# ScalarE's feed-forward work takes other places in the last two row pairs; three VectorE steps move one slot; a class token's energy is written per group

## The chip, the cores and the metric

The kernel runs on one core of one Trainium2 chip. The metric is the device time of one execution in microseconds (us), lower is better. Engines are named TensorE (PE, its weight loads PEld), VectorE (DVE), ScalarE (ACT), GpSimd (POOL) and SyncE (SP, which here only issues DMAs). Each runs its own instructions in order and meets the others at semaphores.

## What is computed

One block of a vision tower over 16 images of 3 x 256 x 256. Sobel magnitudes, summed over the three colours, make 256 tokens of 256 numbers per image; a class token is put in front (S = 257). Then come attention, in which only the 27 tokens of highest energy are queries, and a feed-forward with quantized weights and codes and a depthwise convolution along the tokens.

```python
Ix, Iy = dwconv(x, kx), dwconv(x, ky)             # 3x3 Sobel
h = sum over colours of hypot(Ix, Iy)             # (16, 256, 256)
h = concat([cls_tok, h], axis=1)                  # (16, 257, 256)

z = layernorm(h)                                  # attention
energy = norm(z, axis=-1); _, idx = top_k(energy, 27)
ctx = softmax(q[idx] @ k.T / 4) @ v
result = mean(z, axis=1) everywhere, ctx @ out_w.T + out_b at idx
h = h + result

z = layernorm(h)                                  # feed-forward
g = quantized(z) @ quantized(w1).T                # 257 x 1024 per image
y = silu(depthwise_conv1d(g, conv_w) + conv_b)    # 3 taps along the tokens
h = h + quantized(y) @ quantized(w2).T
```

## The kernel before

**Staging.** The images go in four groups of four (`GB`, `GROUPS`). A group's magnitudes are made in four pairs of rows, i = 0 to 3 (`magnitude_rows`, L797 on VectorE, L1269 on ScalarE). While the magnitudes of group g are made, group g-1 goes through attention (pairs 0 and 1), the residual and the token codes (pair 2) and the feed-forward (pairs 2 and 3). Then VectorE quantizes the hidden values (`ffn_quantize`, L957), normalizes group g (`norm_mean`, `norm_tokens`) and adds the feed-forward's result. There are three such rounds, g = 1, 2, 3; group 0 before them and the last group's attention and feed-forward behind them run without a partner. A round takes about 351 us.

**A pair.** VectorE's part is a long row of steps over 128 x 768 numbers, f = 0 and f = 1 in turn (`hypotenuse`, L678). ScalarE does the absolute values (L1283, L1291, semaphore `mags`), the squares (L1316), the reciprocal roots (L1322, `recips`), the square of the quotient (L1328, `hisq`), the second reciprocal root (L1334, `halfrecip`), and two more squares (L1339, L1344). VectorE waits for each: for `mags` at the pair's start, for `recips` in front of its slot 1 arithmetic, for `hisq` at L746, for `halfrecip` at L753, for L1339's at L759 and for L1344's at L776. In pairs 1 to 3 the gradients are summed by GpSimd's accumulating DMAs (`carried_sums`, L490, the last one L518), which are set off by VectorE's and ScalarE's steps in the pair before.

**Slots.** Between these steps both engines call `slot(k)`, k = -2 to 8 on VectorE and -2 to 9 on ScalarE; other work is put there by hand. On ScalarE slots -2 and -1 stand ahead of the absolute values in pairs 1 to 3, slot 0 ahead of L1316, 1 and 2 behind L1322, 3 and 4 behind L1328, 5 behind L1334, 6 behind L1339, and 7, 8, 9 behind L1344.

**Feed-forward.** An image has 8 tiles of hidden channels, a group 32, numbered i = 0 to 31. TensorE multiplies tile i into PSUM (L1729, here g_i), ScalarE copies it into one of four `gpad` buffers (L1388, the *scale* step, here s_i), TensorE convolves it (L1717, conv_i), ScalarE takes the sum into `ydw` with its bias (L1395, the *take* step, t_i), and after the 8 takes of an image b ScalarE applies silu over all of them (`silu`, L1373, here a_b), whose semaphore `f_ready` VectorE's `hidden_maxima` (L953) waits for. TensorE's order is g_0 to g_3, then conv_0, g_4, conv_1, g_5 and so on: g_i needs s_(i-4), conv_i needs s_i and t_(i-4); s_i needs g_i and conv_(i-4). `FFN_SLOTS` (L38) says in which slot of pair 2 (first table) and pair 3 (second) ScalarE does which of them; an entry is (scale steps, image for silu, take steps). The silu of image 3 stands behind the whole of pair 3 (L1612). Silu and the reciprocal root need different function tables; where they alternate, a table load stands in front of the instruction.

**Attention in pair 1.** VectorE's `own_heads` (L1061) of image 1 is in slot -1. TensorE then picks the image's queries (L1869), and `context` (L1066) copies them at L1069; with it stand `shares` of image 2 and `queries` of image 3. TensorE's last transposes of image 2 (L1850) wait for that copy, and image 3's scores (L1833) wait for them through ScalarE (L1491) and for `queries`.

**Energies.** `select` (L998) finds the 27 highest energies of each image from a row `topk[:, 0, :]`. SP fills it by way of DRAM (L444 to L455): columns 1 to 256 for each group, column 0, the class token's, only for group 0. The row lies in `nrows_mem`, which also holds negated image rows.

Of the kernel before, what the change touches and what calls it, by code (L numbers as in the profile page):

```python
# [22 lines left out]
ACT = mybir.ActivationFunctionType  # L23
# [10 lines left out]
S = H + 1  # L34
# [1 line left out]


FFN_SLOTS = (  # L38
# [6 lines left out]


TILE_SLOTS = tuple((2 * k, 2 * k + 1) for k in range(8)) + ((),)
# [1 line left out]
GB = 4  # L49
# [10 lines left out]
FT = FF // P  # L60
# [66 lines left out]
def tower_kernel(nc, x, cls_tok, w_in, b_qk, b_v, w_out, b_out, w1, conv_w, conv_b, w2, const, out):  # L127
# [11 lines left out]
    with ExitStack() as ctx:  # L139
# [33 lines left out]
        cb = sb("cb", [P, FT])  # L173
# [14 lines left out]
        topk = nrows_mem[0:GB, 0:5 * S].rearrange("p (k n) -> p k n", k=5)  # L188
# [20 lines left out]
        take, again = arena("arena1", 18 * CH * W)  # L209
# [15 lines left out]
        take, again = arena("arena2", FT * ROW9 * P)  # L225
# [37 lines left out]
        gpad = sb("gpad", [P, 4, S + 2])  # L263
# [144 lines left out]
        @block.sync  # L408
        def _(sp):
            def load_weights():  # L410
                sp.dma_start(win[:, :, :], w_in.rearrange("(t p) n -> p t n", p=P)).then_inc(weights_in, 16)
                sp.dma_start(wout[:, :, :], w_out.rearrange("(t p) n -> p t n", p=P)).then_inc(weights_in, 16)

            for b in range(0, GB, 2):
                load_rows(sp, 0, b, 0, 3, img_first)
            sp.dma_start(cst[:, :], const).then_inc(table_in, 16)
            for b in range(0, GB, 2):
                load_rows(sp, 0, b, 3, 4, img_second)
            for b in range(GB):
                load_rows(sp, 0, b, 4, ROWS, img_in)  # L420
                load_rows(sp, 0, b, ROWS, ROWS + 2, img_in)
            sp.dma_start(h9[:, ROWS, :], cls_tok[0:1, :].to_broadcast([P, D])).then_inc(const_in, 16)
            sp.dma_start(stage.rearrange("p (t n) -> p t n", t=DT),
                         w1.rearrange("(t p) n -> p t n", p=P)).then_inc(w1_in, 16)
            sp.dma_start(stage2.rearrange("p (t n) -> p t n", t=FT),
                         w2.rearrange("(t p) n -> p t n", p=P)).then_inc(w2_in, 16)
            load_weights()
            sp.dma_start(bin_col[:, :], b_qk).then_inc(const_in, 16)
            sp.dma_start(bv_col[:, :], b_v).then_inc(const_in, 16)
            sp.dma_start(bo_row[:, :], b_out[0:1, :].to_broadcast([P, D])).then_inc(const_in, 16)  # L430
            sp.dma_start(cw[:, :, :], conv_w).then_inc(const_in, 16)
            sp.dma_start(cb[:, :], conv_b).then_inc(const_in, 16)

            def group(g, first=False, last=False):
                if first:
                    sp.wait_ge(stencil_psum, 2 * ROWS - 3)
                elif not last:
                    sp.wait_ge(mags, g * (2 * PAIRS) + 2 * PAIRS)
                if not last:
                    load_images(sp, g + 1)  # L440
                if not first:

                    sp.wait_ge(f_ready, g * GB)
                    load_weights()  # L444
                if first:

                    sp.wait_ge(e_ready, 1)
                    sp.dma_start(ec_dram, e9[0:1, ROWS:ROW9]).then_inc(e_out, 16)
                    sp.wait_ge(e_out, 16)
                    sp.dma_start(topk[:, 0, 0:1], ec_dram.to_broadcast([GB, 1])).then_inc(erow_in, 16)  # L450

                sp.wait_ge(e_ready, g + 1)
                sp.dma_start(e_dram, e9[:, 0:ROWS]).then_inc(e_out, 16)
                sp.wait_ge(e_out, g * 16 + 32)
                sp.dma_start(topk[:, 0, 1:S], e_dram.rearrange("(b r) j -> b (r j)", b=GB)).then_inc(erow_in, 16)  # L455
                if not first:
                    store(g - 1)

                sp.wait_ge(slots_ready, g + 1)
                sp.dma_start(s_dram.rearrange("(b r) j -> b (r j)", b=GB), topk[:, 4, 1:S]).then_inc(slots_out, 16)  # L460
                if not first:

                    sp.wait_ge(out_done, g * OUT_DONE)
                sp.dma_start(c_dram.rearrange("(b r) o -> b (r o)", b=GB), clsslot[:, :]).then_inc(slots_out, 16)
                sp.wait_ge(slots_out, g * 32 + 32)
                sp.dma_start(slot9[:, 0:ROWS], s_dram).then_inc(slot9_in, 16)
                sp.dma_start(slot9[:, ROWS:ROW9], c_dram).then_inc(slot9_in, 16)

            def store(g):

                sp.wait_ge(out_ready, g + 1)
                for b in range(GB):
                    sp.dma_start(out[bass.ds(g * GB + b, 1), 1:S, :].rearrange("o (p r) d -> (o p) r d", r=ROWS),
                                 out9[b * BLK:(b + 1) * BLK, 0:ROWS, :]).then_inc(out_done, 16)
                sp.dma_start(out[bass.ds(g * GB, GB), 0, :], out9[0:P:BLK, ROWS, :]).then_inc(out_done, 16)

            group(0, first=True)
            for g in range(1, GROUPS - 1):
                group(g)
            group(GROUPS - 1, last=True)  # L480
            store(GROUPS - 1)
            sp.wait_ge(out_done, GROUPS * OUT_DONE)
# [63 lines left out]
        def _(dve):  # L546
# [451 lines left out]
            def select(step, g):  # L998

                er, ew, tk, eq, slot = (topk[:, k, :] for k in range(5))  # L1000
                gt, cum = tk, ew
                dve.wait_ge(erow_in, g * 16 + 32)
                src = er
                for k in range(4):
                    settle()
# [130 lines left out]
            def slots_1(step, g):  # L1136
                def slot(k):
                    if k == -2: score_maxima(step, g, 2)
                    if k == -1: own_heads(step, g, 1)
                    if k == 0:  # L1140
                        context(step, g, 1)
                        shares(step, g, 2)
                        queries(step, g, 3)
                    if k == 2: score_maxima(step, g, 3)
                    if k == 3: own_heads(step, g, 2)
                    if k == 4:
                        context(step, g, 2)
                        shares(step, g, 3)
                    if k == 7: own_heads(step, g, 3)
                    if k == 8: context(step, g, 3)  # L1150
                return slot
# [89 lines left out]
        def _(act):  # L1241
# [136 lines left out]
                act.wait_ge(f_ready, gf * GB + b + 1)  # L1378
                s.activation(idle[:, half:half + 1], clsT[:, 0:1], ACT.Copy)

            def ffn_take(gf, scale, image, take):

                nt = gf * (GB * FT)
                for i in scale:
                    if i >= 4:
                        act.wait_ge(conv_psum, nt + i - 3)
                    act.wait_ge(g_psum, nt + i + 1)
                    s.activation(gpad[:, i % 4, 1:S + 1], (A0, A1, B0, B1)[i % 4][:, 0:S], ACT.Copy).then_inc(gd_ready, 1)  # L1388
                if image is not None:
                    act.wait_ge(conv_taken, nt + (image + 1) * FT)  # L1390
                    silu(gf, image, image % 2)
                for i in take:
                    t = i % FT
                    act.wait_ge(conv_psum, nt + i + 1)
                    s.activation(ydw[:, t, :], (C0, C1, T0, T1)[i % 4][:, 0:S], ACT.Identity,  # L1395
                                 bias=cb[:, t:t + 1]).then_inc(conv_taken, 1)

            def tap_diagonals(tiles):

# [168 lines left out]
            def slots_2(g):  # L1568
                def slot(k):
                    if k == 0: residual_sums(g)  # L1570
                    if k == 1:
                        tokens_scaled(g)
                        tap_diagonals(range(4, FT))
                    if k in FFN_SLOTS[0]:
                        ffn_take(g, *FFN_SLOTS[0][k])
                return slot

            def slots_3(g):
                def slot(k):
                    if k in FFN_SLOTS[1]:  # L1580
                        ffn_take(g, *FFN_SLOTS[1][k])
                return slot

            for lo, hi_, landed in ((0, 3, img_first), (3, 4, img_second)):
# [21 lines left out]
            for g in range(1, GROUPS):  # L1606
# [2 lines left out]
                magnitude_rows(g, 1, slots_1(gl))  # L1609
                magnitude_rows(g, 2, slots_2(gl), lambda: residual_squares(gl))  # L1610
                magnitude_rows(g, 3, slots_3(gl))
                ffn_take(gl, (), GB - 1, ())  # L1612
                norm_squares(lambda j: ln[0][:, j, :], d_ready, g, ROWS)
                ffn_scales(gl)
                first_root(g, ROWS)
# [352 lines left out]
```

## Time and profile before

| | |
|---|---|
| median of 3 runs | 1550.82 us (1550.23 to 1552.83) |
| profiled execution, device time | 1551.41 us |
| profiled execution, span | 1549.6 us |
| VectorE busy | 1319.3 us (85%) |
| TensorE matmul busy | 819.3 us (53%), weight loads 647.0 us |
| ScalarE busy | 718.5 us (46%) |
| GpSimd busy | 167.4 us (11%) |

The profile is one execution; the span runs from its first to its last instruction, 1.8 us less than the device time around it. Busy shares are means over stages with different limits, so they only say where to look. A line of the waits has the waiting engine and line, what released it, the us in total, how often, and the longest. A line of the timeline has the start, the us up to the last end of the run of like instructions, engine, line, operation, output and input, and in brackets how long the engine sat idle before it and what ended that. Neighbouring instructions overlap by some 0.1 us, so from start to start is a little less than a duration. On TensorE each fp32 multiplication of the program stands as two in the records, so "x6" at L1717 is one convolution (3 taps) and "x4" at L1729 one g_i. A line of the windows view has a stretch, its length, the busy us and instructions of PE, PEld, DVE, ACT and POOL, the granted TensorE clock as a share of 2.4 GHz, the share of the DMA engines and GB/s. Most times below are of the middle round, g = 2.

### The profile page before, as it was taken

To read this page: it belongs to the slowest core of one execution; us is meant where nothing else is said; L and a number is where in the kernel's file an instruction comes from. 1 tells how busy PE (TensorE), PEld (TensorE's weight loads), DVE (VectorE), ACT (ScalarE), POOL (GpSimd) and SP (SyncE) were. 2 spreads that over 40 slices of the span, in tenths; PEclk is the share of its full clock that TensorE was granted. 3 is DMA by queue.
4 is the path that set the end of the run, shared out by engine and by line. 5 is a ranking of instruction groups with operands and counts; after the bars stand their busy time and mean duration, and the time that the engine had idled before them with its cause. 6 is when DMAs were issued, how large, how long until landed. Compare 5 with 4: busy or idle time off the path is not lost.

```text
span 1549.6 us, 11187 instructions
## 1 busy us (share of the span) xinstructions
PE 819.3 (53%) x3334; PEld 647.0 (42%) x3334; DVE 1319.3 (85%) x2024; ACT 718.5 (46%) x1294; POOL 167.4 (11%) x208
## 2 busy tenths in 40 slices
PE   3465100467647733556648643456648633586534
PEld 1233000345546522445537533345537532475423
DVE  7999998898996999998997899998998799522576
ACT  2212242255486534255475644156476544243662
POOL 0000000022313000012303000012303000000000
PEclk8787555757679876667679876567579876688876
DMA  8000600034717510125618510116527010100001
GB/s 201 3 11 14 116 0 0 1 60 76 120 25 127 103 41 0 28 48 89 103 33 133 106 41 1 28 31 105 92 44 130 7 41 1 28 1 1 0 0 27
DMA packets 46356, 78.13 MB, mean 50 GB/s; under 512 B 7466, under 2 KB 31706, under 8 KB 44634
## 3 DMA queue, kind: packets, MB, share of 16 engines
q0 software_dynamic: 33408, 50.34, 20.0%
q1 hardware_dynamic: 12314, 26.31, 7.4%
q10 hardware_dynamic: 576, 0.79, 0.2%
q8 instruction: 26, 0.43, 0.1%
q14 instruction: 32, 0.26, 0.1%
HBM read 22.84 MB, written 4.25 MB: 17 GB/s over the span
## 4 chain that ended last, share of the span: by engine, by line
DVE 45%; ACT 14%; PE 13%; issue 8%; DMA 5%; POOL 0%; SPq 0%; DVEq 0%; ACTq 0%
DVE arena L564 15%; DVE arena L567 13%; ACT arena L1376 3%; DVE arena L953 3%; PE psum L1717 2%; PE psum L1811 2%; DMA arena<-nrows_mem 2%; DMA arena<-zT 2%; ACT arena L1249 2%; PE psum L1833 1%; DMA arena<-img 1%; DVE red L580 1%; ACT arena L1513 1%; PE psum L1786 1%; PE psum L1729 1%
## 5 line engine op out<-in xcount | busy, mean ns | idle before, releaser
L564 DVE TENSOR_TENSOR arena<-arena 128x768 f32<-128x768 f32 (+2 forms) x519 | 475.9, 968 | 58.2 <-ACT arena L1291 50.8
L567 DVE SCALAR_TENSOR_TENSOR arena<-arena 128x768 f32<-128x768 f32 (+2 forms) x224 | 201.5, 949 | 0.1
L1729 PE MATMUL psum<-zT,w1q 128*128 128x257 f32 x512 | 138.8, 405 | 21.0 <-DVE gpad L948 16.0
L1729 PEld LDWEIGHTS psum<-zT,w1q 128*128 128x128 f32 x512 | 103.0, 204 | 43.4 <-DVE gpad L948 20.9
L1717 PE MATMUL psum<-gpad,win 128*128 128x257 f32 x288 | 78.3, 411 | 47.8 <-ACT gpad L1388 47.8
L1833 PE MATMUL psum<-arena 128*128 128x257 f32 x128 | 55.0, 604 | 90.5 <-ACT arena L1491 72.1
L540 POOL DMA_DIRECT2D h<-others x60 | 51.5, 859 | 436.6 <-DVE others L567 357.0
L1328 ACT ACTIVATE arena<-arena 128x768 f32<-128x768 int16 x32 | 27.0, 844 | 154.1 <-DVE arena L567 153.7
L1717 PEld LDWEIGHTS psum<-gpad,win 128*128 128x128 f32 x288 | 57.4, 205 | 63.7 <-ACT gpad L1388 53.8
L1249 ACT ACTIVATE arena<-arena 128x256 f32<-128x256 f32 x65 | 23.3, 409 | 127.2 <-DVE arena L567 68.2
L1833 PEld LDWEIGHTS psum<-arena 128*128 128x128 f32 x128 | 36.8, 301 | 102.5 <-ACT arena L1491 75.8
L567 DVE SCALAR_TENSOR_TENSOR arena<-img 128x768 f32<-128x768 f32 x74 | 67.4, 948 | 9.1 <-DMA img<-x 8.7
L501 POOL DMA_DIRECT2D arena<-nrows_mem x18 | 15.6, 865 | 505.3 <-ACT arena L1300 433.0
L953 DVE TENSOR_REDUCE arena<-arena 128x288 f32<-128x2304 f32 (+1 forms) x16 | 64.3, 4078 | 0.1
L1395 ACT ACTIVATE xT<-psum,cb 128x257 f32<-128x257 f32 x96 | 42.7, 477 | 38.0 <-PE psum L1717 38.0
L1481 ACT ACTIVATE arena<-psum,arena 128x257 f32<-128x257 f32 x64 | 29.5, 474 | 65.3 <-DVE arena L1052 65.3
L1717 PE MATMUL psum<-gpad,onehotT 128*128 128x257 f32 x216 | 55.7, 400 | 7.5 <-ACT gpad L1388 7.5
L567 DVE SCALAR_TENSOR_TENSOR arena<-arena,others 128x768 f32<-128x768 int16 x64 | 58.2, 950 | 0.0
L1861 PE MATMUL psum<-arena 128*128 128x64 f32 x256 | 56.6, 362 | 2.8 <-ACT arena L1491 2.8
L1664 PE MATMUL psum<-img,cst 128*128 128x512 f32 (+1 forms) x28 | 16.0, 713 | 74.1 <-DVE arena L567 63.4
L1376 ACT ACTIVATE arena<-xT 128x2048 f32<-128x2048 f32 (+1 forms) x14 | 55.0, 3932 | 0.3
L1777 PE MATMUL psum<-cst,arena 128*128 128x128 f32 x64 | 15.6, 408 | 73.3 <-DVE e L564 71.2
(235 smaller groups left out, 2109.6 us busy)
## 6 DMA issues: line engine op xcount, KB each, us to landing
arena<-nrows_mem POOLq DMA_DIRECT2D x36, 384.0 KB, 7.7
arena<-img POOLq DMA_DIRECT2D x36, 384.0 KB, 7.6
img<-x SPq DMA_DIRECT2D x36, 258.0 KB, 7.0
h<-others POOLq DMA_DIRECT2D x60, 128.0 KB, 2.7
arena<-arena POOLq DMA_DIRECT2D x18, 384.0 KB, 8.8
arena<-zT POOLq DMA_DIRECT2D x12, 384.0 KB, 8.4
out<-out SPq DMA_DIRECT2D x16, 256.0 KB
img<-x SPq DMA_DIRECT2D x48, 64.5 KB, 6.7
```

Source lines behind the costliest of these rows:

```text
L540: pool.dma_start(h9[:, row, :], others[:, row % 2, c, :], accum_op=ALU.add).then_inc(row_sums, 16)
L564: return v.tensor_tensor(o, a, b, op)
L567: return v.scalar_tensor_tensor(out=o, in0=a, scalar=s, in1=b, op0=op0, op1=op1)
L953: return v.tensor_reduce(fmax[:, :, bass.ds(b, 1), :].rearrange("p j o r -> p j (o r)"), f4[:, :, :, bass.ds(b, 1), :].rearrange("p t j o ...
L1249: ins = s.activation(ln[1][:, j, :], src(j), ACT.Square)
L1376: s.activation(fb[:, :, 0:ROWS, :], yd[:, :, 1:S].rearrange("p t (r j) -> p t j r", j=ROWS), ACT.Silu)
L1395: s.activation(ydw[:, t, :], (C0, C1, T0, T1)[i % 4][:, 0:S], ACT.Identity, bias=cb[:, t:t + 1]).then_inc(conv_taken, 1)
L1717: ins = mm((C0, C1, T0, T1)[i % 4][:, 0:S], diagonal(t, k), gpad[:, i % 4, k:k + S], start=(k == 0), stop=(k == 2))
L1729: ins = mm((A0, A1, B0, B1)[i % 4][:, 0:S], w1q[:, k, t * P:(t + 1) * P], zT[:, k, b, :], start=(k == 0), stop=(k == DT - 1))
L1811: ins = mm(C0[:, t * P:(t + 1) * P], y_row(j)[:, t * P:(t + 1) * P], rhs, start=(j == 0), stop=(j == ROWS))
L1833: mm((C0, C1, T0, T1)[hg][:, 0:S], qbd[:, hg // 2, 4 * (hg % 2):4 * (hg % 2) + 4, :].rearrange("p h q -> p (h q)"), kT[:, b % 2, hg // 2, ...
L1861: mm(B1[:, chans], attnT[:, f, m, cols], V[:, b % 2, m, chans], start=(m == 0), stop=False)
```

## The change

1. `FFN_SLOTS` becomes a written order of single steps ("s13 t10 s14 ..."), and `ffn_take` goes through it. Of pair 2, slot 5 is empty now and slot 9 too; by its end 13 scale and 10 take steps are done, where it was 16 and 14. Of pair 3, slots -2, -1 and 0 are empty; slot 1 has six tiles and the silu of image 1, slot 3 four tiles, slot 6 three tiles, slot 7 the rest with the silu of images 2 and 3. The call behind pair 3 is gone, since `a3` is in slot 7.
2. On VectorE in pair 1, `context` of image 1, `shares` of image 2 and `queries` of image 3 move from slot 0 to slot 1, behind eight steps of the pair.
3. SP writes the class token's energy into column 0 for every group, ahead of the DMA that sends the other energies; `select` waits for both.

```diff
--- before.py
+++ after.py
@@ -36,12 +36,10 @@
 
 
 FFN_SLOTS = (
-    {2: ((0, 1, 2, 3), None, ()), 3: ((4, 5), None, (0, 1)), 4: ((6,), None, (2, 3)), 5: ((7,), None, (4, 5)),
-     6: ((8, 9), None, (6, 7)), 7: ((10, 11), 0, (8, 9)), 8: ((12, 13), None, (10, 11)), 9: ((14, 15), None, (12, 13))},
-    {-2: ((), None, (14, 15)), -1: ((), 1, ()),
-     0: ((16, 17), None, ()), 1: ((18, 19), None, (16, 17)), 2: ((20, 21, 22), None, (18, 19)),
-     3: ((23,), None, (20, 21, 22)), 4: ((24,), None, (23,)), 6: ((25, 26), 2, (24,)),
-     7: ((27, 28, 29), None, (25, 26)), 8: ((30, 31), None, (27, 28, 29)), 9: ((), None, (30, 31))})
+    {2: "s0 s1 s2 s3", 3: "t0 s4 t1 s5 t2 s6", 4: "t3 s7", 6: "t4 s8 t5 s9 t6 s10", 7: "t7 s11 a0", 8: "t8 s12 t9"},
+    {1: "s13 t10 s14 t11 s15 t12 s16 t13 s17 t14 s18 t15 a1", 3: "t16 s19 t17 s20 t18 s21 t19 s22",
+     6: "t20 s23 t21 s24 t22 s25",
+     7: "t23 a2 s26 t24 s27 t25 s28 t26 s29 t27 s30 t28 s31 t29 t30 t31 a3"})
 
 
 TILE_SLOTS = tuple((2 * k, 2 * k + 1) for k in range(8)) + ((),)
@@ -447,9 +445,9 @@
                     sp.wait_ge(e_ready, 1)
                     sp.dma_start(ec_dram, e9[0:1, ROWS:ROW9]).then_inc(e_out, 16)
                     sp.wait_ge(e_out, 16)
-                    sp.dma_start(topk[:, 0, 0:1], ec_dram.to_broadcast([GB, 1])).then_inc(erow_in, 16)
 
                 sp.wait_ge(e_ready, g + 1)
+                sp.dma_start(topk[:, 0, 0:1], ec_dram.to_broadcast([GB, 1])).then_inc(erow_in, 16)
                 sp.dma_start(e_dram, e9[:, 0:ROWS]).then_inc(e_out, 16)
                 sp.wait_ge(e_out, g * 16 + 32)
                 sp.dma_start(topk[:, 0, 1:S], e_dram.rearrange("(b r) j -> b (r j)", b=GB)).then_inc(erow_in, 16)
@@ -999,7 +997,7 @@
 
                 er, ew, tk, eq, slot = (topk[:, k, :] for k in range(5))
                 gt, cum = tk, ew
-                dve.wait_ge(erow_in, g * 16 + 32)
+                dve.wait_ge(erow_in, g * 32 + 32)
                 src = er
                 for k in range(4):
                     settle()
@@ -1137,7 +1135,7 @@
                 def slot(k):
                     if k == -2: score_maxima(step, g, 2)
                     if k == -1: own_heads(step, g, 1)
-                    if k == 0:
+                    if k == 1:
                         context(step, g, 1)
                         shares(step, g, 2)
                         queries(step, g, 3)
@@ -1378,22 +1376,23 @@
                 act.wait_ge(f_ready, gf * GB + b + 1)
                 s.activation(idle[:, half:half + 1], clsT[:, 0:1], ACT.Copy)
 
-            def ffn_take(gf, scale, image, take):
+            def ffn_take(gf, work):
 
                 nt = gf * (GB * FT)
-                for i in scale:
-                    if i >= 4:
-                        act.wait_ge(conv_psum, nt + i - 3)
-                    act.wait_ge(g_psum, nt + i + 1)
-                    s.activation(gpad[:, i % 4, 1:S + 1], (A0, A1, B0, B1)[i % 4][:, 0:S], ACT.Copy).then_inc(gd_ready, 1)
-                if image is not None:
-                    act.wait_ge(conv_taken, nt + (image + 1) * FT)
-                    silu(gf, image, image % 2)
-                for i in take:
+                for what, i in [(w[0], int(w[1:])) for w in work.split()]:
                     t = i % FT
-                    act.wait_ge(conv_psum, nt + i + 1)
-                    s.activation(ydw[:, t, :], (C0, C1, T0, T1)[i % 4][:, 0:S], ACT.Identity,
-                                 bias=cb[:, t:t + 1]).then_inc(conv_taken, 1)
+                    if what == "s":
+                        if i >= 4:
+                            act.wait_ge(conv_psum, nt + i - 3)
+                        act.wait_ge(g_psum, nt + i + 1)
+                        s.activation(gpad[:, i % 4, 1:S + 1], (A0, A1, B0, B1)[i % 4][:, 0:S], ACT.Copy).then_inc(gd_ready, 1)
+                    elif what == "t":
+                        act.wait_ge(conv_psum, nt + i + 1)
+                        s.activation(ydw[:, t, :], (C0, C1, T0, T1)[i % 4][:, 0:S], ACT.Identity,
+                                     bias=cb[:, t:t + 1]).then_inc(conv_taken, 1)
+                    else:
+                        act.wait_ge(conv_taken, nt + (i + 1) * FT)
+                        silu(gf, i, i % 2)
 
             def tap_diagonals(tiles):
 
@@ -1572,13 +1571,13 @@
                         tokens_scaled(g)
                         tap_diagonals(range(4, FT))
                     if k in FFN_SLOTS[0]:
-                        ffn_take(g, *FFN_SLOTS[0][k])
+                        ffn_take(g, FFN_SLOTS[0][k])
                 return slot
 
             def slots_3(g):
                 def slot(k):
                     if k in FFN_SLOTS[1]:
-                        ffn_take(g, *FFN_SLOTS[1][k])
+                        ffn_take(g, FFN_SLOTS[1][k])
                 return slot
 
             for lo, hi_, landed in ((0, 3, img_first), (3, 4, img_second)):
@@ -1609,7 +1608,6 @@
                 magnitude_rows(g, 1, slots_1(gl))
                 magnitude_rows(g, 2, slots_2(gl), lambda: residual_squares(gl))
                 magnitude_rows(g, 3, slots_3(gl))
-                ffn_take(gl, (), GB - 1, ())
                 norm_squares(lambda j: ln[0][:, j, :], d_ready, g, ROWS)
                 ffn_scales(gl)
                 first_root(g, ROWS)
```

## Rows read from the trace of the kernel before

**Rows 1.** The page's first part: busy time, share of the span, instructions.
```profile
PE 819.3 (53%) x3334; PEld 647.0 (42%) x3334; DVE 1319.3 (85%) x2024; ACT 718.5 (46%) x1294; POOL 167.4 (11%) x208
```

**Rows 2.** VectorE's waits over the whole span: total, times, longest.
```profile
DVE arena L564 <- ACT arena L1291: 50.8, 7, 16.1
DVE arena L1069 <- PE psum L1869: 31.2, 7, 5.7
```

**Rows 3.** VectorE's timeline, pair 3 and what follows: start, length, line, idle before.
```profile
858.63 3.56 DVE L564 TENSOR_TENSOR arena<-arena 128x768 f32<-128x768 f32 x4 [16.10 <-ACT arena L1291]
...
885.64 1.82 DVE L567 SCALAR_TENSOR_TENSOR arena<-arena 128x768 f32<-128x768 f32 x2
...
897.69 1.82 DVE L564 TENSOR_TENSOR arena<-arena 128x768 f32<-128x768 f32 x2 [1.22 <-ACT arena L1344]
...
910.71 11.99 DVE L953 TENSOR_REDUCE arena<-arena 128x288 f32<-128x2304 f32 x3
```

**Rows 4.** ScalarE's timeline over the end of pair 2 and pair 3.
```profile
840.54 0.82 ACT L1395 ACTIVATE xT<-psum,cb 128x257 f32<-128x257 f32 x2
...
851.99 3.87 ACT L1376 ACTIVATE arena<-xT 128x2048 f32<-128x2048 f32 x1
...
879.67 1.71 ACT L1328 ACTIVATE arena<-arena 128x768 f32<-128x768 int16 x2 [8.44 <-DVE arena L567]
...
886.62 1.71 ACT L1334 ACTIVATE arena<-arena 128x768 f32<-128x768 f32 x2 [2.52 <-DVE arena L567]
...
890.77 1.28 ACT L1376 ACT_TABLE_LOAD   x1
892.07 3.96 ACT L1376 ACTIVATE arena<-xT 128x2048 f32<-128x2048 f32 x1
...
896.47 0.46 ACT L1395 ACTIVATE xT<-psum,cb 128x257 f32<-128x257 f32 x1
...
908.59 3.94 ACT L1376 ACTIVATE arena<-xT 128x2048 f32<-128x2048 f32 x1
```

**Rows 5.** TensorE's timeline in pair 3, and last one stretch of the windows view.
```profile
859.65 2.94 PE L1717 MATMUL psum<-gpad,win 128*128 128x257 f32 x6 [7.33 <-ACT gpad L1388]
862.38 1.92 PE L1729 MATMUL psum<-zT,w1q 128*128 128x257 f32 x4
864.10 2.29 PE L1717 MATMUL psum<-gpad,win 128*128 128x257 f32 x6
866.22 1.03 PE L1729 MATMUL psum<-zT,w1q 128*128 128x257 f32 x4
867.09 1.46 PE L1717 MATMUL psum<-gpad,win 128*128 128x257 f32 x6
...
859.00:865.00 6.00, 5.35 (x13) 4.24 (x14) 6.00 (x9) 5.97 (x11) 0.00 (x0) 0.50 0.84 180
```

**Rows 6.** Timeline: GpSimd's last accumulating DMA for pairs 2 and 3, its user in pair 2.
```profile
771.28 0.86 POOL L518 DMA_DIRECT2D arena<-nrows_mem  x1 [1.18 <-DMA arena<-zT]
...
836.75 0.86 POOL L518 DMA_DIRECT2D arena<-nrows_mem  x1 [1.34 <-DMA arena<-h]
...
779.70 0.84 ACT L1291 ACTIVATE arena<-arena 128x768 f32<-128x768 f32 x1 [1.05 <-DMA arena<-nrows_mem]
```

**Rows 7.** Timelines of VectorE, ScalarE and TensorE in pair 1.
```profile
721.40 0.23 DVE L1069 COPY arena<-psum 128x64 f32<-128x64 f32 x1 [4.72 <-PE psum L1869]
...
734.25 1.22 DVE L1051 TENSOR_REDUCE arena<-psum 128x4 f32<-128x1028 f32 x1
...
719.67 1.58 ACT L1291 ACTIVATE arena<-arena 128x768 f32<-128x768 f32 x2
...
730.14 3.79 PE L1833 MATMUL psum<-arena 128*128 128x257 f32 x8 [7.43 <-ACT arena L1491]
```

**Rows 8.** SP's column-0 DMA (one line's answer: ns min/median/max), and select in the tail.
```profile
L450 SPq DMA_DIRECT2D nrows_mem<-ec_dram x1: 243/243/243, 270.0 to 270.0; - x1
...
1328.85 0.41 DVE L1006 MAX8 best<-nrows_mem 4x8 f32<-4x257 f32 x1
```

## The prediction

> **What bounds the kernel now.** First the busy times [rows 1]: VectorE works 85% of the span and no other engine much over half, so an edit pays mainly where VectorE stands still. Then VectorE's waits, longest in total first [rows 2]. At the top stands its wait for L1291, the absolute values at the start of a pair: 50.8 us in seven waits, the longest 16.1. Then VectorE's timeline over pair 3 [rows 3]: it sits idle for 16.10 us before it starts at 858.63. The same wait of 16.10 us stands in front of pair 3 in each of the three rounds, 48.3 of the 50.8 us. What ScalarE does meanwhile is in its timeline [rows 4]: take steps from 840.54 that wait for TensorE, then the silu of image 1 from 851.99, and only then the absolute values that VectorE wants. Pair 3 itself has one more wait, 1.22 us at 897.69, behind the silu of image 2 (892.07) that stands ahead of L1344. So in each round some 17 us of VectorE's time hang on where ScalarE's feed-forward steps stand, and the reader should see that this work isn't too much for ScalarE, it stands in the wrong place for VectorE.
>
> **Pair 2 to pair 3.** In the new order ScalarE has, behind the silu of image 0 (unmoved, done where the takes at 840.54 start [rows 4]), only t8, s12 and t9, at some 0.36 us each: 896.47 to the next step is such a take. It is free at about 841.7. What comes last then is GpSimd's sum. In pair 2 its last DMA was issued at 771.28 and its user began at 779.70 with no other cause to wait, 8.42 us later [rows 6]. The one for pair 3 is issued at 836.75 [rows 6], and nothing of the edit reaches it, since its inputs come from slots 4 to 6 of pair 2 and six short steps in slot 6 (2.1 us) end before L1344 is due. So the second absolute value starts at 845.17 and VectorE has it at 846.05. Before, the second step of VectorE's run began one step of 0.87 behind 858.63, at 859.50 [rows 3]. VectorE is **13.45 us** earlier. All times below marked "new" carry this shift, in the middle round.
>
> **Slot 1 of pair 3.** It begins when L1316, a table load of 1.28 and L1322 are done: maximum ready at new 846.9, squares to 847.8, load to 849.1, roots to 850.8 (a pair of such steps takes 1.7, as at L1334 [rows 4]). TensorE has stood since about 845.7 for want of s13 (s12 gave it conv_12 and g_16, again at the lower clock, from 841.4). What it does after such idle time is in its timeline [rows 5]: conv 2.73 from start to start, g 1.72, conv 2.12, then 0.87 and 1.30 (a record of 1.46 overlaps the next by 0.16). The granted clock over those six us is 0.50, the lower level of 1.2 GHz, after an idle time of 7.33 us [rows 5]; the steps that follow at half the length are at 2.4. The long steps cost 3.1 us over the steady pace of 2.17 a tile. conv_13 starts 0.4 behind s13, at 851.2; conv_15 ends 8.74 later at 859.9; t15 and the silu of image 1 with its load follow (890.77 to 896.47, 5.7 us [rows 4]), to 866.1. VectorE's quotient, and with it L1328, was at 879.67, new 866.22 [rows 4]: just in time, and its answer is not due before VectorE's 885.64, new 872.2 [rows 3]. Four microseconds of cover; hidden.
>
> **Slots 3 and 6.** ScalarE leaves L1328 at 867.9. Six of the eight steps find TensorE's work done (conv_18 and g_22 end by 867.3); t19 waits for conv_19, started on s19, to 870.2, and s22 ends at 870.9. The table load that the silu of image 1 has made necessary ends at 872.2. L1334 is due at 886.62 - 13.45 = 873.17 [rows 4]. Cover 1.0 us, the thinnest place: every us that TensorE takes over my 3.1 falls on VectorE. In slot 6 the silu is gone, six steps are done at 878.8, and L1344 isn't due before VectorE's L772, which ended at 896.47 (897.69 less 1.22 [rows 3]), new 883.0 for the second half. The 1.22 us wait goes too. VectorE's first maximum, which ends at 910.71 [rows 3] and takes 4.03, begins at 906.68, so VectorE's pair 3 ends at new 906.68 - 13.45 - 1.2 = 892.0.
>
> **Slot 7 and the last silu.** This is where part of the gain is given back. L1344 leaves ScalarE at 883.8. t23 and the silu of image 2 take 6.1, so s26 starts at 889.9 and TensorE, idle again for 5 us, starts conv_26 at 890.3. Behind it stand g_30, conv_27, g_31 and conv_28 to 31: 2.73 + 1.72 + 2.12 + 0.87 + 4 x 1.30 = 12.64 us [rows 5], to 903.0. t31 ends at 903.5, and the silu of image 3 without a load takes 4.3 (3.94 [rows 4] and the class token's 0.4): 907.8. VectorE's first three maxima take 4.03 each [rows 3] and end at 904.1. It waits 3.8 us, and the fourth ends at 911.9. Before, it ended at 910.71 + 11.99 = 922.70 [rows 3]. **Gain 10.8 us a round.** GpSimd's sums for pair 3 need some 12 us behind VectorE's end of the pair and stay under those maxima.
>
> **The three moved VectorE steps.** In pair 1 VectorE waits 4.72 us for TensorE's L1869 [rows 7], once a round; the other four of the seven waits [rows 2] are in the tail, which is unchanged. But the next step needs L1291 of that pair, which begins at 719.67 [rows 7] and gives the first half at 720.5. So the wait moves there rather than goes: VectorE starts its maxima at 720.5 instead of 1.5 us behind 721.40 (the three steps take that), and does those 1.5 later. The gain is 721.40 less 720.45, **0.95 us**. What is late next: image 3's scores. Their PE run starts at 730.14 today [rows 7] and is wanted at 734.25. The copy now comes at about 726.6; transposes, ScalarE's L1491 and the scores end near 732.4, wanted at 733.3. Bounds: a loss of 1 us, and a gain of the whole 4.72 if the absolute values came first. I take 0.95, because both releasers are rows.
>
> **The class token's energy.** One more DMA issue of 0.24 us [rows 8] on SP ahead of the others, four small packets; groups 1 and 2 have select some 13 us behind the energies. In the tail select starts at 1328.85 without idle time [rows 8], so there is little cover: 0 to 0.24 us once. I take 0.1.
>
> **Table loads.** Silu of image 1 between the two reciprocal roots makes two more loads a round. In the rows a load takes 1.28 and the next instruction follows at 1.30 (890.77 to 892.07 [rows 4]); that is what I counted. The Trainium skill ("ScalarE: Activation LUTs", What ACT_TABLE_LOAD costs) speaks against this change: it adds a drain of about 1.38 us to each switch and advises to do all of one set first. By that page's figure both loads would reach L1334's cover of 1.0, an estimate of 1.8 us more a round, 5 us in all. The row shows no such gap, so I leave it out.
>
> **The sum.** 3 x (10.8 + 0.95) - 0.1 = 35.2 us. The profiled span of 1549.6 becomes 1514.4. The median is 1550.82 (the profiled execution, at 1551.41, lay 0.6 over it), so the time becomes **1515.6**.
>
> **Rivals and their times.**
> (a) *Likeliest, 0.64:* as worked out, VectorE waits for the last silu. Own range: from no cost of the lower clock at all in slot 7 (3.1 us a round less, 1506) to half of (c)'s loss, 1523.
> (b) *VectorE-bound, 0.06:* the last silu is in time too; another 3.8 us a round: 1504. For it: the cost of the lower clock differs from idle to idle. Against: 3.8 is more than all of it.
> (c) *TensorE pays twice, 0.20:* the lower clock costs 6.2 instead of 3.1 in each block, or the next group's images, now loaded 13 us earlier, meet GpSimd's row sums and delay L753. Then 3.1 more in slot 7 and 3.1 - 1.0 at L1334: 5.2 us a round, 1531.
> (d) *Slower, 0.06:* TensorE stays at its lower level through pair 3, because ScalarE now feeds it in bursts with stops of 5 us between. At 2.6 a conv and 1.72 a g, L1334 is some 8 late, slots 6 and 7 add some 5, and the last block takes 19 instead of 12.6: the fourth maximum ends about 11 us later than now, less 0.95, and the time is 1581. It decides from the point where the last silu ends later than 919.6, against my 907.8. Against it: in rows 5 the clock is back within three groups.
> (e) *The change doesn't do it, 0.04:* GpSimd's sum for pair 3 lands 13 us later than its issue says, since today nobody waits for it there and its landing is not shown by a wait; VectorE idles as before and the time stays at 1550.
>
> **Range and chances.** 1506 to 1530 takes in (a) and most of (c) and leaves out about 0.2. Faster by over 0.2% (3.1 us, about what a measurement of this kernel can tell from no change): (a), (b), (c), 0.90. Within 0.2%: (e), 0.04. Slower: (d), 0.06.
>
> **What would show it.** In the new profile: the wait for L1291 in front of pair 3 under 4 us, ending at GpSimd's DMA; no wait at L776; no or hardly a wait at L755 for L1334; a new wait of VectorE's fourth L953 for ScalarE's silu, near 4 us a round; L1069 without a wait and L1291's in pair 1 at some 4 us; three table loads for silu a round instead of two, and one more at L1334. The prediction is wrong if VectorE waits for halfrecip or for the fourth maximum by more than 5 us each, or if the granted clock stays at 0.50 for long stretches in which ScalarE waits for TensorE.

## The result and the profile after

The changed kernel takes **1518.24 us** (median of 4, 1514.93 to 1519.31) against 1551.59 us (median of 4) for the kernel before on the same chip: a ratio of 0.9782, 95% interval 0.9764 to 0.9800. That is 33.4 us less, where 35.2 were worked out, and inside the range of 1506 to 1530. A second measurement of the same kernel (r1b below) gave 1516.46 against 1551.85 us, ratio 0.9774 (0.9758 to 0.9790), 35.4 us less. The profiled execution took 1519.31 us, the longest of the four, with a span of 1517.5.

Line numbers above 44 are two lower in the changed kernel up to `ffn_take`: L1291 is L1289, L953 is L951, L1069 is L1067, L1334 is L1332. From `ffn_take` on, the scale step stands at L1388, the take step at L1391, silu at L1374, the convolution at L1715 and g_i at L1727. First VectorE's waits over the whole span (total, times, longest), which answer to [rows 2]:

```profile
DVE arena L562 <- ACT arena L1289: 22.5, 13, 3.9
DVE arena L1067 <- PE psum L1867: 17.1, 4, 6.6
DVE arena L951 <- ACT arena L1375: 8.5, 3, 3.7
```

The wait for the absolute values went from 50.8 us in seven to 22.5 in thirteen, none over 3.9. The one in pair 1 for TensorE's L1867 is gone (the four left are in the tail, which is what follows the third round: the last group's attention and feed-forward). A new line stands third: the fourth maximum waits for the last silu, once a round. VectorE's timeline of the middle round's pair 3 answers to [rows 3]:

```profile
829.23 0.06 DVE L552 MEMSET idle<- 128x1 f32 x1
831.02 0.96 DVE L562 TENSOR_TENSOR arena<-arena 128x768 f32<-128x768 f32 x1 [1.73 <-ACT arena L1289]
832.94 2.70 DVE L562 TENSOR_TENSOR arena<-arena 128x768 f32<-128x768 f32 x3 [0.96 <-ACT arena L1289]
...
859.06 1.83 DVE L565 SCALAR_TENSOR_TENSOR arena<-arena 128x768 f32<-128x768 f32 x2
...
878.99 4.08 DVE L951 TENSOR_REDUCE arena<-arena 128x288 f32<-128x2304 f32 x1
...
894.85 4.02 DVE L951 TENSOR_REDUCE arena<-arena 128x288 f32<-128x2304 f32 x1 [3.69 <-ACT arena L1375]
898.79 3.61 DVE L572 TENSOR_REDUCE red<-h 128x128 f32<-128x2048 f32 x1
```

Where 16.10 us stood in front of the pair there are 1.73 and 0.96. The pair has no wait inside, and 3.69 us come back in front of the fourth maximum. ScalarE's timeline shows why the first two are there and how close slot 3 is (answers to [rows 4, 6]):

```profile
828.01 0.48 ACT L1391 ACTIVATE xT<-psum,cb 128x257 f32<-128x257 f32 x1
828.37 1.58 ACT L1281 ACTIVATE arena<-arena 128x768 f32<-128x768 f32 x2
830.14 0.84 ACT L1289 ACTIVATE arena<-arena 128x768 f32<-128x768 f32 x1 [0.19 <-DMA arena<-nrows_mem]
832.06 0.84 ACT L1289 ACTIVATE arena<-arena 128x768 f32<-128x768 f32 x1 [1.07 <-DMA arena<-nrows_mem]
...
857.95 0.47 ACT L1391 ACTIVATE xT<-psum,cb 128x257 f32<-128x257 f32 x1 [1.21 <-PE psum L1715]
858.33 0.38 ACT L1388 ACTIVATE gpad<-psum 128x257 f32<-128x257 f32 x1
858.72 1.28 ACT L1332 ACT_TABLE_LOAD   x1
860.06 1.71 ACT L1332 ACTIVATE arena<-arena 128x768 f32<-128x768 f32 x2
```

Of VectorE's first wait (1.73 us) only 0.19 us is the landing of GpSimd's last sum, the rest is the last take and ScalarE's own absolute values. In front of the second absolute value ScalarE itself stands idle for 1.07 us until the sum has landed. No feed-forward work but that one take stands in the way any more. And TensorE's timeline, which answers to [rows 5]: a convolution of pair 2, then the block of slot 1, conv_19 of slot 3, and the start of the last block.

```profile
816.03 1.57 PE L1715 MATMUL psum<-gpad,win 128*128 128x257 f32 x6 [2.24 <-ACT gpad L1388]
...
838.17 2.94 PE L1715 MATMUL psum<-gpad,onehotT 128*128 128x257 f32 x6 [5.91 <-ACT gpad L1388]
...
846.00 1.03 PE L1727 MATMUL psum<-zT,w1q 128*128 128x257 f32 x4
...
855.51 2.40 PE L1715 MATMUL psum<-gpad,win 128*128 128x257 f32 x6 [1.98 <-ACT gpad L1388]
857.71 1.92 PE L1727 MATMUL psum<-zT,w1q 128*128 128x257 f32 x4
...
877.27 2.94 PE L1715 MATMUL psum<-gpad,win 128*128 128x257 f32 x6 [4.63 <-ACT gpad L1388]
```

### The profile page after: what moved, and what is told of

It reads as the page before. It is cut to its first block, busy times and chain, and to the rows that moved or that the text cites. A ratio compares the mean times of both kernels' runs of the same rounds, so it can differ in the third digit from the quotient of the medians.

```text
span 1517.5 us, 11197 instructions
## 1 busy us (share of the span) xinstructions
PE 815.9 (54%) x3334; PEld 645.1 (43%) x3334; DVE 1320.9 (87%) x2024; ACT 728.9 (48%) x1300; POOL 166.2 (11%) x208
## 4 chain that ended last, share of the span: by engine, by line
DVE 45%; ACT 12%; DMA 10%; PE 10%; issue 7%; POOL 0%; SPq 0%; DVEq 0%; ACTq 0%
DVE arena L562 16%; DVE arena L565 14%; DMA arena<-nrows_mem 3%; DMA arena<-img 3%; ACT arena L1374 2%; PE psum L1715 2%; PE psum L1809 2%; DMA arena<-h 2%; DMA arena<-zT 2%; ACT arena L1247 2%; DVE red L578 1%; ACT arena L1512 1%; DVE arena L951 1%; DVE arena L1049 1%; DVE out L565 1%
## 5 line engine op out<-in xcount | busy, mean ns | idle before, releaser
L562 DVE TENSOR_TENSOR arena<-arena 128x768 f32<-128x768 f32 (+2 forms) x519 | 477.4, 975 | 26.3 <-ACT arena L1289 22.5
L1727 PE MATMUL psum<-zT,w1q 128*128 128x257 f32 x512 | 142.2, 414 | 19.4 <-DVE gpad L946 14.8
L1727 PEld LDWEIGHTS psum<-zT,w1q 128*128 128x128 f32 x512 | 105.4, 208 | 42.9 <-DVE gpad L946 19.9
L538 POOL DMA_DIRECT2D h<-others x60 | 52.4, 873 | 375.2 <-DVE others L565 286.1
L1715 PE MATMUL psum<-gpad,win 128*128 128x257 f32 x288 | 77.1, 406 | 26.1 <-ACT gpad L1388 26.1
L1715 PE MATMUL psum<-gpad,onehotT 128*128 128x257 f32 x216 | 58.0, 413 | 31.0 <-ACT gpad L1388 31.0
L1715 PEld LDWEIGHTS psum<-gpad,win 128*128 128x128 f32 x288 | 57.3, 202 | 38.7 <-ACT gpad L1388 29.8
L951 DVE TENSOR_REDUCE arena<-arena 128x288 f32<-128x2304 f32 (+1 forms) x16 | 64.9, 4098 | 8.7 <-ACT arena L1375 8.5
L1391 ACT ACTIVATE xT<-psum,cb 128x257 f32<-128x257 f32 x96 | 45.5, 474 | 40.7 <-PE psum L1715 40.7
L1715 PEld LDWEIGHTS psum<-gpad,onehotT 128*128 128x128 f32 x216 | 44.3, 208 | 40.8 <-ACT gpad L1388 33.7
L1374 ACT ACTIVATE arena<-xT 128x2048 f32<-128x2048 f32 (+1 forms) x14 | 55.2, 3941 | 0.2
```

The source lines that it names most:

```text
L538: pool.dma_start(h9[:, row, :], others[:, row % 2, c, :], accum_op=ALU.add).then_inc(row_sums, 16)
L562: return v.tensor_tensor(o, a, b, op)
L951: return v.tensor_reduce(fmax[:, :, bass.ds(b, 1), :].rearrange("p j o r -> p j (o r)"), f4[:, :, :, bass.ds(b, 1), :].rearrange("p t j o ...
L1374: s.activation(fb[:, :, 0:ROWS, :], yd[:, :, 1:S].rearrange("p t (r j) -> p t j r", j=ROWS), ACT.Silu)
L1715: ins = mm((C0, C1, T0, T1)[i % 4][:, 0:S], diagonal(t, k), gpad[:, i % 4, k:k + S], start=(k == 0), stop=(k == 2))
L1727: ins = mm((A0, A1, B0, B1)[i % 4][:, 0:S], w1q[:, k, t * P:(t + 1) * P], zT[:, k, b, :], start=(k == 0), stop=(k == DT - 1))
```

## Experiments

Time alone mixes two things here, so each profiled execution was also read at one mark, the first MAX8 of `select` in the last group. What lies ahead of it holds the three rounds, what lies behind is the tail, whose instructions no edit touches.

| kernel | median us | ratio (95%) | mark, us | tail, us |
|---|---|---|---|---|
| before | 1551.59 | | 1328.85 | 220.8 |
| changed | 1518.24 | 0.9782 (0.9764 to 0.9800) | 1293.22 | 224.3 |
| changed, again (r1b) | 1516.46 | 0.9774 (0.9758 to 0.9790) | 1292.00 | 220.8 |
| e1, order only | 1520.15 | 0.9804 (0.9788 to 0.9821) | 1297.19 | 220.7 |
| e2, the two other parts only | 1548.54 | 0.9983 (0.9974 to 0.9993) | 1325.73 | 221.6 |
| e3, silu of image 1 only | 1538.62 | 0.9925 (0.9908 to 0.9941) | 1316.36 | 219.5 |
| e4, two scale steps ahead | 1505.07 | 0.9711 (0.9695 to 0.9727) | 1283.49 | 219.7 |
| e5b, images later | 1515.32 | 0.9768 (0.9752 to 0.9784) | 1292.85 | 220.8 |
| e6b, exponentials later | 1499.95 | 0.9650 (0.9628 to 0.9672) | 1274.15 | 224.2 |

Each ratio is to the kernel before on the same chip: 1550.98 us beside e1 to e4, 1551.85 beside e5b, e6b and r1b.

**e1: the order alone.** The edit against the changed kernel, shortened:

```diff
-                    if k == 1:
+                    if k == 0:
                         context(step, g, 1)
...
-                sp.dma_start(topk[:, 0, 0:1], ...)      # for every group
+                    sp.dma_start(topk[:, 0, 0:1], ...)  # back under "if first"
...
-                dve.wait_ge(erow_in, g * 32 + 32)
+                dve.wait_ge(erow_in, g * 16 + 32)
```

> The change with only ScalarE's new feed-forward order: VectorE's three steps of pair 1 stay in slot 0 and the class token's energy is written for group 0 alone, as before. My theory: this order carries 32 to 33 us of the gain (10.8 us a round worked out, VectorE's wait in front of pair 3 from 16.1 to about 2.7 us, a new wait of 2.4 to 3.7 us for the last silu), so about 1552 - 32 = 1520 us; the wait for L1869 in pair 1 is back at 4.4 to 4.7 us. Rival: the moved VectorE steps matter more than 1 us a round; then this kernel stays 8 us or more over the changed one, at 1526 or above.

Measured 1520.15 us. The mark is 31.7 us earlier than before, 10.6 a round. The order carries nearly all of the gain, and the wait for L1867 in pair 1 is back, 6.0, 4.4 and 4.7 us in the three rounds. The rival falls: by the ratios this kernel is 3.4 us over the changed one in its first measurement and 4.7 in its second, not 8.

**e2: the two other parts alone.** The edit against the kernel before, shortened:

```diff
-                    if k == 0:
+                    if k == 1:
                         context(step, g, 1)
...
-                    sp.dma_start(topk[:, 0, 0:1], ...)  # under "if first"
+                sp.dma_start(topk[:, 0, 0:1], ...)      # for every group
...
-                dve.wait_ge(erow_in, g * 16 + 32)
+                dve.wait_ge(erow_in, g * 32 + 32)
```

> The kernel before with only the two other parts: the three VectorE steps in slot 1 of pair 1, and the class token's energy written for each group. My theory: the 4.7 us wait for L1869 turns into one of about 3.9 for the absolute values, 0.8 to 0.95 us a round, so 2.5 to 3 us faster than before, 1549; the extra DMA shows no wait at select. Rival 1: the moved steps give the whole 4.7 us a round, 1537. Rival 2: the scores of image 3 are late and VectorE waits at the score maxima instead, no gain, 1552.

Measured 1548.54 us, 2.6 less by the ratio (0.0017 x 1551), and 3.1 at the mark. VectorE's waits in it:

```profile
DVE arena L564 <- ACT arena L1291: 60.5, 9, 16.1
DVE arena L1069 <- PE psum L1869: 17.0, 4, 6.6
```

Against [rows 2], the wait for L1869 lost three of its seven and 14.2 us, while that for L1291 grew by 9.7. VectorE now waits 3.87 us for the absolute values in pair 1 of each round. The wait moved rather than went, as worked out. Rival 1 falls, and rival 2 too, since VectorE has no new wait at L1051. How the 3.1 us divide between the two parts no run shows; `select` starts without a wait here too.

**e3: only the silu of image 1 moves.** The edit against the kernel before:

```diff
-    {-2: ((), None, (14, 15)), -1: ((), 1, ()),
-     0: ((16, 17), None, ()), 1: ((18, 19), None, (16, 17)), ...
+    {-2: ((), None, (14, 15)),
+     0: ((16, 17), None, ()), 1: ((18, 19), 1, (16, 17)), ...
```

> The kernel before with one edit: the silu of image 1 goes from slot -1 to slot 1 of pair 3, between the scale and the take steps there. My theory: of the 16.1 us that VectorE waits in front of pair 3, this silu is 4.3 (from 851.99 to 856.31), and the rest is the take steps paced by TensorE; so the wait falls to about 11.8 us and the time by 3 x 4.3 = 13 us, 1539. Rival: the silu alone held the pair up (then the wait falls under 4 us and the time to about 1520), or its two added table loads eat the gain (1550).

Measured 1538.62 us, and the wait in front of pair 3:

```profile
DVE arena L564 <- ACT arena L1291: 34.1, 7, 11.7
```

16.1 became 11.7, and the mark came 12.5 us earlier, 4.2 a round. So a quarter of the wait was this silu. Most of the rest is take steps paced by TensorE: in the middle round of this trace ScalarE stands idle for TensorE in front of the last four of them, 6.9 us in all. Behind them stand only the absolute values themselves. The two more table loads a round found room: no new wait of VectorE shows up.

**e4: TensorE gets work for the time of the silu.** The edit against the changed kernel:

```diff
-     7: "t23 a2 s26 t24 s27 t25 s28 t26 s29 t27 s30 t28 s31 t29 t30 t31 a3"})
+     7: "t23 s26 s27 a2 t24 s28 t25 s29 t26 s30 t27 s31 t28 t29 t30 t31 a3"})
```

> The changed kernel with s26 and s27 ahead of the silu of image 2 in slot 7 of pair 3, where they stand behind it. TensorE then has conv_26, g_30, conv_27 and g_31 to do while ScalarE does that silu, and doesn't stand still for 4.6 us and start at the lower clock. My theory: the last silu ends some 5 us earlier in relation to VectorE's pair 3, VectorE's wait at the fourth maximum (2.5, 3.7, 2.4 us in the three rounds) goes, and the time falls by 8.6 us to about 1510. Rival: the last silu is bound by ScalarE's own work and the order doesn't matter, 1518.

Measured 1505.07 us, 5 under what was expected, and no wait of VectorE at L951 among its waits any more. The mark is 9.7 us earlier than in the changed kernel's first profile and 8.5 earlier than in its second, whose three waits at L951 come to 8.5 and 8.4 us. So the last silu was late because TensorE had stood still behind `a2`, not because ScalarE had too much to do. By the ratios the gain is 11.0 us against the changed kernel's first measurement (0.9782 less 0.9711, of 1551) and 9.8 against its second, more than the waits. Part of that is the tail, which in e4's profile is 4.6 and 1.1 us shorter than in the changed kernel's two; see r1b.

**e5b: the next images' load later.** The edit against the changed kernel:

```diff
-                    sp.wait_ge(mags, g * (2 * PAIRS) + 2 * PAIRS)
+                    sp.wait_ge(hisq, g * (2 * PAIRS) + 2 * PAIRS)
```

> The changed kernel with SP's load of the next group's images started at L1326 of pair 3 instead of L1289, some 21 us later. In the changed kernel's trace that load runs beside GpSimd's row sums of pair 2, whose DMAs then take up to 10.4 us to land (5.0 at most before the change), and the last of them ends 5.6 us before VectorE's L751 of pair 3 needs it. My theory: the sums' longest landing falls to about 5 us again and the time doesn't move (within 2 us of the changed kernel's 1518), since VectorE had cover. Rival: the traffic also costs VectorE and ScalarE time, its 128x768 steps being some 7 ns longer each in the changed kernel; then 2 us or more are gained.

Measured 1515.32 us, 1516.46 for the changed kernel beside it: the same. How long GpSimd's row sums (L538) took from issue to landing, first in the changed kernel, then here:

```profile
DMA to landing us min/median/max: 2.6/2.7/10.4
```

```profile
DMA to landing us min/median/max: 2.6/2.7/4.3
```

The collision of rival (c) is real and was covered. The rival about VectorE's steps falls: the plain 128x768 step took 954 ns here, 954 and 956 in the changed kernel's two profiles, 950 before. Nor is it the change that makes them longer, since they took 951 in e4, which has all of it. What those 4 to 6 ns come from stays open. Over all steps of 128x768 they come to 2.6 us in the changed kernel's second profile and 3.5 in its first, which is a term that the prediction didn't have.

**r1b: the changed kernel once more.**

> The changed kernel once more, unaltered, for its tail. From select of the last group to the end the profiled executions took 220.8 us (before), 224.3 (after), 220.7, 221.6, 219.5 and 219.7 (the four experiments), with the same instructions. My theory: this stretch is bound by TensorE, and its length depends on where the granted clock stands at its lower level in that execution, not on the change; the tail here comes out between 219 and 225 again, and the stretch before it is 1293.2 us within 0.5. Rival: the change makes the tail some 3.5 us longer always, so 224 again.

The tail took 220.8 us, not 224.3, with the same instructions. The first 95 us of the tail in the windows view, in the first profile and in this one (busy us and instructions of PE, PEld, DVE, ACT, POOL, then the granted clock):

```profile
1293.22:1388.22 95.00, 76.75 (x353) 64.45 (x353) 23.46 (x66) 25.25 (x64) 0.00 (x0) 0.78 0.05 12
```

```profile
1292.00:1387.00 95.00, 80.78 (x371) 67.40 (x371) 23.53 (x66) 28.10 (x78) 0.00 (x0) 0.80 0.05 12
```

TensorE gets through 353 and through 371 instructions in the same time. The largest part of that gap opens in ten microseconds some 40 us behind the mark, again in the first profile and in this one:

```profile
1333.22:1343.22 10.00, 10.00 (x30) 8.29 (x31) 0.56 (x2) 2.88 (x10) 0.00 (x0) 0.50 0.00 0
```

```profile
1332.00:1342.00 10.00, 9.24 (x47) 7.62 (x46) 1.83 (x6) 4.72 (x14) 0.00 (x0) 0.83 0.00 0
```

TensorE is busy throughout at the lower level in the first, and does 30 multiplications there against 47. So the rival falls, and the tail's length hangs on the execution and not on the change. That the granted clock makes it fits all nine profiles, but is read from them and not tried: e3 and e4, with the shortest tails, have 0.83 over the 95 us, e6b, with 224.2, has the 0.78 and the 353 instructions of the first profile. The mean alone doesn't give the length, since e2 has 0.78 too and a tail of 221.6; it matters which stretch the lower level falls on. The mark missed my 0.5 us: 1292.00 against 1293.22, so the rounds too vary by a microsecond. What places the lower level in one execution and not in another stays open.

**e6b: a version beyond both.** On top of e4:

```diff
-                    if k == -2: exponentials(g, 2)
-                    if k == 0:
+                    if k == 0: exponentials(g, 2)
+                    if k == 1:
                         keys(g, 3)
                         values(g, 3)
-                    if k == 1: weights_transposed(g, 2)
+                        weights_transposed(g, 2)
```

> The kernel with s26 and s27 ahead of the silu of image 2 (1505 us), and in pair 1 ScalarE's exponentials of image 2 move from slot -2, ahead of the absolute values, to slot 0 behind them, and keys and values of image 3 from slot 0 to slot 1. VectorE waits 3.9 us a round there now for absolute values that stand behind the exponentials (1.9 us) and whose sums have landed before VectorE is there. My theory: that wait goes, at most 0.5 us is lost at the reciprocal roots, and the time falls by 3 x 3.2 to about 1496. Rival: image 3's scores come late, VectorE waits at its score maxima, and the gain is under 1 us a round, 1502 or more.

Measured 1499.95 us, 3.5% under the kernel before, 4 over the 1496 that was expected. By the ratios it is 9.5 us under e4 (0.9711 less 0.9650), and the mark is 9.3 us ahead of e4's, where 9.6 were expected; its profiled tail was a long one, 4.5 us over e4's. VectorE's pair 1 begins without a wait:

```profile
698.07 0.42 DVE L562 TENSOR_TENSOR arena<-psum,arena 128x256 f32<-128x256 f32 x1
698.41 3.55 DVE L562 TENSOR_TENSOR arena<-arena 128x768 f32<-128x768 f32 x4
```

## Why the prediction was right, and where not

The prediction was right in its mechanism as well as in the number: each wait that it named went, moved or came where it said. The steps of the middle round, in order. To set shifts of this round apart from those before it, I take the start of the token codes' maximum, 785.94 before and 772.69 after, as zero: 13.25 us are older.

- **Pair 2 to pair 3.** Worked out 13.45. The second step of VectorE's run began at 859.50 and begins at 832.94: 26.56, less 13.25, is 13.3. What releases the absolute value in front of it is the sum's landing, as said; rival (e) falls.
- **Slot 1.** The block from conv_13 to the end of conv_15 takes 838.17 to 846.00, 7.8 where I had 8.74: the lower clock cost 2.2, not 3.1. Hidden either way.
- **Slot 3.** Here my cover was wrong, in this round. I had 1.0 us between the end of the table load and L1332's due time. In the trace the load ends at 860.00 and L1332 starts 1.00 behind VectorE's 859.06, as it did before (0.98, [rows 3, 4]). The cover is some 0.05. The reason is conv_19: from start to start it took 2.20 (855.51 to 857.71) after an idle time of 1.98 us, and I had counted the lower clock in slots 1 and 7 only. In rounds 1 and 3 of the same profile conv_19 took 1.40 and ScalarE stood idle for 0.89 us in front of L1332, which is the cover that I had. That the middle round lost nothing is luck: in e1 and e4, where conv_19 took 2.52 and 2.59 in the middle round, VectorE waited 0.33 and 0.39 us for L1332.
- **The silu of image 2 leaves slot 6.** The 1.22 us at L1342's user are gone. VectorE's first maximum began at 906.68 and begins at 878.99: 27.7 less 13.25 is 14.4, worked out 14.65.
- **The last silu.** Worked out a wait of 3.8 in front of the fourth maximum; measured 3.69 here, 2.5 and 2.4 in the other rounds, where TensorE came back to its higher clock sooner (the lower one cost the last block 3.1 us here, as in my rows, and 1.9 and 1.8 there). The block from conv_26 to t31's start takes 877.27 to 890.13, 12.9, worked out 12.8. Net gain to the end of the maxima: 922.70 less 898.87 is 23.8, less 13.25, is **10.6; worked out 10.8**.
- **The three moved steps.** Worked out 0.95 a round, measured 1.04 alone (e2: 3.12 over three rounds) and 1.3 or 1.7 beside the new order (1297.19 less 1293.22 or 1292.00, over three). Both take in the energy's DMA.
- **The energy's DMA.** L450 takes 0.27 us of SP for the last group, and `select` starts with no idle time behind it.
- **Table loads.** In the changed kernel 11 for silu and 9 at L1332, where it was 8 and 6, so two more a round. Where ScalarE waits for nothing else, a load and its successor start 1.29 to 1.34 us apart (858.72 to 860.06). The Trainium skill ("ScalarE: Activation LUTs", What ACT_TABLE_LOAD costs) adds a drain of about 1.38 us to each; this trace doesn't show it. With a cover of 0.05 at L1332, the drain's 1.38 would have shown on VectorE as a wait.
- **The sum.** 35.2 worked out; at the mark 35.6 and 36.9 in the two profiles. By the first MAX8 of `select` in each round, the first profile gains 11.85, 11.96 and 11.82 us where 11.75 a round were worked out. The second gains 12.0, 13.5 and 11.4, so a match to a tenth in one round is partly luck. The term that my sum lacked is the tail. I held it for fixed, and it moved by 3.5 us between executions of one kernel; the first profile had a long one. That can account for the 1.8 us between 35.2 and 33.4, but isn't shown: the medians' own executions have no trace.
- **The range.** Rival (c)'s own time, 1531, lay outside the range of 1506 to 1530 that was said to take in most of (c). The result doesn't depend on it.

Rival (d), TensorE at its lower clock through pair 3, didn't come: the clock was back after one to three groups of steps in each block. Rival (b) didn't come in this kernel, but e4 is exactly it, made by an edit: 3.8 us a round more was my price, 2.8 to 3.2 was measured.

## What to carry to other kernels

When the busiest engine waits for a helper, look at what the helper does in its queue ahead of the awaited step, and move it to a place where the busy engine has a long run of its own; then work out what is late next. A run of steps that another engine paces (here TensorE's 2.17 us a tile) needs a place as long as its pace, not as its own work. And before a helper goes into a long step, let it first release whatever it already can, so that the third engine has work meanwhile: that was worth another quarter of the change (e4: 8.5 to 9.7 us at the mark beside 35.6 to 36.9).

## What was not expected of the hardware

- The tail of 220 us, in which TensorE is busy for 133 to 137, took 219.5 to 224.3 us over nine profiles with the same instructions in it; where TensorE's lower level fell differed between them.
- An idle time of 1.98 us was enough once for steps at the lower level (2.20 for a convolution, from start to start), while one of 2.24 us in pair 2 left them at the higher one (1.57 lasting, 1.40 to the next). Over the 18 rounds of the six profiles with the new order, conv_19 went slower in eight, after idle times of 1.87 to 2.17 us, and at the higher level in ten, after 1.15 to 1.65 and once 2.64. The idle time in front of a step alone doesn't tell which it will be.
- GpSimd's accumulating DMAs of 128 KB landed after up to 10.4 us beside the load of four images, where 2.7 is the median, and after 4.3 at most with the load moved away.
